# A four-layer graph network: the second layer's boundary rows put at their nodes by one-hots on chip, and its last chunk worked off in parts

## The reference, cut to what matters

```python
xn = x * rsqrt(sum(x * x, -1) + eps)
att = beta[0] * sum(xn[row_index] * xn[col_index], -1)        # one number per edge
m = segment_max(att, row_index)
e = exp(att - m[row_index])
denom = segment_sum(e, row_index)
alpha = e / maximum(denom[row_index], 1e-16)
out = segment_sum(alpha[:, None] * x[col_index], row_index)   # [6250, 64]
x = layernorm(x + out)
```

## Time and profile before

| what | value |
|---|---|
| runs | 4829.73, 4836.84, 4835.64 us; median 4835.64 us |
| the profiled execution | 4837.0 us, its span 4835.0 us |
| busy share of the span | POOL 73%, DVE 58%, PE 30%, ACT 23% |
| second layer, edge stage | 1201 to 2258 us |
| second layer, mend and node stage | 2258 to 2399 us |
| third layer, edge stage | 2399 to 3560 us |
| fourth layer, edge stage | 3706 to 4758 us |

### The profile page before, as it was taken

One profiled execution on the slowest core, in us unless ns is written; L12 is line 12 of the kernel. 1 busy time (PEld: TensorE's weight loads), 2 busy tenths in 40 slices (PEclk: granted clock), 3 DMA queues, 4 the chain that ended last, 5 costly groups with the idle time before them and its releaser, 6 DMA issues.

```text
span 4835.0 us, 31278 instructions
## 1 busy us (share of the span) xinstructions
PE 1465.4 (30%) x6525; PEld 744.2 (15%) x6525; DVE 2821.7 (58%) x7339; ACT 1123.2 (23%) x3417; POOL 3549.3 (73%) x3637
## 2 busy tenths in 40 slices
PE   7722100000000000000588888888834010000003
PEld 3611100000000000000233333333324010000002
DVE  4688632224555555555368888888866444444445
ACT  2200000000000000000278888888844000000000
POOL 6777777777777777776777777777734777777776
PEclk9855555555555555555799999999966555555555
DMA  7222222221222222222135555555532222222222
GB/s 279 72 95 96 86 78 79 79 73 50 69 80 80 80 80 80 80 80 60 59 124 213 196 199 213 191 203 213 199 137 61 78 78 78 78 78 78 79 78 75
DMA packets 185543, 529.64 MB, mean 110 GB/s; under 512 B 70422, under 2 KB 74634, under 8 KB 169080
## 3 DMA queue, kind: packets, MB, share of 16 engines
q1 hardware_dynamic: 65384, 395.51, 21.7%
q0 software_dynamic: 117728, 129.84, 11.7%
q10 hardware_dynamic: 2224, 2.13, 0.1%
HBM read 185.57 MB, written 341.47 MB: 109 GB/s over the span
## 4 chain that ended last, share of the span: by engine, by line
POOL 54%; issue 19%; DVE 9%; PE 7%; DMA 6%; ACT 4%; POOLq 0%; SPq 0%; DVEq 0%; ACTq 0%
POOL AR L190 52%; DMA AR<-xt,Si 4%; DVE AR L514 3%; POOL xd L194 2%; PE ps L680 2%; ACT AR L1306 2%; DMA AR<-y,R 1%; ACT AR L1168 1%; PE ps L1161 1%; PE ps L587 1%; PE ps L1177 1%; DVE AR L1290 1%; DVE AR L364 1%; DVE AR L366 1%; PE ps L372 0%
## 5 line engine op out<-in xcount | busy, mean ns | idle before, releaser
L190 POOL DMA_INDIRECT AR<-xt,Si x2496 | 2429.0, 973 | 809.6 <-issue 747.0
L190 POOL DMA_INDIRECT AR<-y,R x752 | 722.1, 960 | 237.4 <-issue 217.9
L1161 PE MATMUL ps<-AR,WLR 128*128 128x512 f32 x1248 | 626.8, 627 | 18.3 <-ACT AR L1168 18.3
L1320 DVE SCALAR_TENSOR_TENSOR AR<-AR,gf 128x390 f32<-128x390 f32 x780 | 484.6, 621 | 148.5 <-ACT AR L1306 132.7
L1306 ACT ACTIVATE AR<-AR 128x64 f32<-128x64 f32 x1664 | 498.5, 349 | 0.0
L514 DVE SCALAR_TENSOR_TENSOR AR<-AR,gf 128x64 f32<-128x64 f32 x831 | 237.4, 286 | 365.5 <-DMA AR<-y,R 337.6
L1595 DVE TENSOR_TENSOR AR<-AR,ps 128x2048 f32<-128x2048 f32 (+1 forms) x53 | 119.1, 2247 | 541.4 <-DMA AR<-xt,Si 541.4
L1168 ACT ACTIVATE AR<-ps 128x512 f32<-128x512 f32 x624 | 370.9, 595 | 80.5 <-PE ps L1161 78.4
L958 PE MATMUL ps<-AR,ones 128*128 128x384 f32 (+1 forms) x6 | 3.7, 759 | 1201.1 <-DVE AR L910 1201.1
L797 DVE TENSOR_TENSOR AR<-AR,ps 128x512 f32<-128x512 f32 x104 | 66.9, 684 | 443.9 <-DMA AR<-xt,Si 443.9
L1605 DVE SCALAR_TENSOR_TENSOR AR<-AR,gf 128x128 f32<-128x128 f32 x831 | 294.0, 354 | 29.5
(11 more groups left out here) (308 smaller groups left out, 2895.1 us busy)
## 6 DMA issues: line engine op xcount, KB each, us to landing
s<-AR SPq DMA_DIRECT2D x51, 3168.0 KB, 10.7
AR<-xd SPq DMA_DIRECT2D x104, 512.0 KB
s<-AR SPq DMA_DIRECT2D x51, 1024.0 KB, 4.0
AR<-xt,Si POOLq DMA_INDIRECT x2496, 2.5
s<-AR SPq DMA_DIRECT2D x52, 528.0 KB, 3.1
s<-AR SPq DMA_DIRECT2D x53, 512.0 KB, 2.7
xd<-AR SPq DMA_DIRECT2D x52, 512.0 KB
y<-AR SPq DMA_DIRECT2D x24, 1024.0 KB, 4.1
```

What stands on the lines that cost most here:

```text
L190: g.indirect_dma_start(out=o, out_offset=None, in_=table, in_offset=bass.IndirectOffsetOnAxis(ap=idx, axis=0)).then_inc(S[sem], 16)
L1161: t.matmul(PS[2 + k % 3][:], WLR[:, ch * P:(ch + 1) * P], XT2[:, u % 6, :], start=True, stop=True).then_inc(S["pm"], 1)
L1320: m = v.scalar_tensor_tensor(out=Sv[:, j, 0:HW], in0=Sv[:, j - 1, 0:HW], scalar=gf[:, c * CH + j:c * CH + j + 1], in1=Sv[:, j, 0:HW], op0= ...
```

## The change

`mend_soft_g` is split. The second layer keeps only the row gather, and its node gathers follow it in POOL's queue. The node rows of partition-crossing nodes are replaced on chip: `ends_v` makes, in the edge stage at chunk 20, one-hots of the partition's first node (`KE`, `LOE`) and the mask `has1` of the node slots that have a mended row; `ended_v` spreads the mended row over the slots, `ended_t` moves it with `KE` to the partition that owns the node, `ended_a` copies it from PSUM, and `nodes1_v` puts it over the gathered row with a predicated copy. In the last chunk the second half of the gathers has its own semaphore, the steps of the chunk before it run ahead of its `soft1` work, and it is stored in four parts of 4 columns. The third layer keeps its scatter. Counts of semaphores are adapted.

```diff
--- before.py
+++ after.py
@@ -61,13 +61,13 @@
 
 
 
-    late = 16 * CH // 2 if L and b == (NCH - 1) % N0 else 0
+    late = 16 * CH // 2 * min(L, 2) if b == (NCH - 1) % N0 else 0
     return sum(16 * CH // h * len(range(b // h, NCH, n)) for n, h in ((N0, 1), (4, 1), (NX, 2), (4, 1))[0:L] if b // h < n) - late
 
 
 def stored_before(L, b):
 
-    late = (16 if L and b == (NCH - 1) % N0 else 0) + (48 if L > 2 and b == (NCH - 1) % 2 else 0)
+    late = sum(m for l, (m, n) in enumerate(((16, N0), (48, 3), (48, 2))[0:L]) if b == (NCH - 1) % n)
     return sum(16 * len(range(b, NCH, n)) for n in (N0, 3, 2, 3)[0:L] if b < n) + late
 
 
@@ -111,7 +111,7 @@
                  "zrow"]
         names += [f"f{k}{n}" for k in range(2) for n in ("v", "io", "cn", "pe", "pos", "sc", "ld", "zt", "xs")]
         names += [f"{n}{k}" for k in range(2) for n in ("hoh", "hpe", "cnt", "rv", "rp")]
-        names += ["tl", "late", "lin0", "lin3", "rz", "rt", "ra", "ry", "rb", "rc"]
+        names += ["el", "ep", "ec", "tl", "late", "lin0", "lin3", "rz", "rt", "ra", "ry", "rb", "rc"]
         names += [f"g_{i}" for i in range(2 * NX)] + [f"s_{i}" for i in range(N0)] + [f"x_{i}" for i in range(3)]
         names += [f"ys{i}" for i in range(4)] + [f"nod_{i}" for i in range(2)]
         S = {n: ctx.enter_context(nc.semaphore("k_" + n)) for n in names}
@@ -612,7 +612,7 @@
                     v.copy_predicated(o, m_, y).then_inc(S["rc"], 1)
 
         def stored_all(e, L, n):
-            more = (16, 0, 48, 16)[L]
+            more = (16, 48, 48, 16)[L]
             for b in range(n):
                 e.wait_ge(S[f"s_{b}"], stored_before(L, b) + 16 * len(range(b, NCH, n)) + (more if b == (NCH - 1) % n else 0))
 
@@ -755,7 +755,8 @@
             if c >= 4:
                 e.wait_ge(S["p1"], 2 * (c - 3))
             for j in range(CH):
-                gather(G1[:, c % 4, j * 65:(j + 1) * 65], xt1, Si[:, c * CH + j:c * CH + j + 1], f"g_{c % 4}")
+                gather(G1[:, c % 4, j * 65:(j + 1) * 65], xt1, Si[:, c * CH + j:c * CH + j + 1],
+                       "late" if c == NCH - 1 and j >= CH // 2 else f"g_{c % 4}")
 
         def x1_chunk(e, c):
             if c >= 3:
@@ -792,7 +793,9 @@
                 e.wait_ge(S["q1"], n)
             if i == 0:
                 e.wait_ge(S["f1"], 16 * (c + 1))
-                e.wait_ge(S[f"g_{c % 4}"], gathered_before(1, c % 4) + 16 * CH * (c // 4 + 1))
+                e.wait_ge(S[f"g_{c % 4}"], gathered_before(1, c % 4) + 16 * CH * (c // 4 + 1) - (16 * CH // 2 if c == NCH - 1 else 0))
+            if i == 1 and c == NCH - 1:
+                e.wait_ge(S["late"], 16 * CH)
             if i <= 1:
                 m = v.tensor_tensor(TM1[:, 8 * i:8 * i + 8, :], Gv[:, 8 * i:8 * i + 8, 0:D],
                                     PS[2 * (c % 2) + i][:].rearrange("p (j d) -> p j d", j=8), ALU.mult)
@@ -848,6 +851,54 @@
                                    scalar=gf[:, c * CH + j:c * CH + j + 1] if j else pf1[:, c % 2, CH:CH + 1],
                                    in1=Sv[:, j, 0:65], op0=ALU.mult, op1=ALU.add).then_inc(S["t1"], 1)
 
+
+
+
+        KE = arena(15400, P)
+        LOE = arena(15600, NL)
+        has1 = arena(15700, NL).bitcast(I32)
+        TL1 = arena(16000, NG, GN * 65)
+        CP1 = arena(20000, NG, GN * 65)
+        ramp1 = arena(15000, P)
+        upto1 = arena(15200, P)
+        ke, keq, kel = sm[:, 17:18], sm[:, 18:19], sm[:, 19:20]
+
+        def ends_v(e, c):
+            c.hold()
+            v.tensor_scalar(ramp1, ident[:], pf, None, op0=ALU.mult).then_inc(S["el"], 1)
+            c.then(lambda: v.tensor_tensor(ke, df_, inv, ALU.subtract))
+            e.wait_ge(S["ep"], 1)
+            c.then(lambda: v.tensor_scalar(upto1, PS[5][:, 0:P], float(NL), ke, op0=ALU.mult, op1=ALU.is_le))
+            c.then(lambda: v.reduce_sum(keq, upto1, AX))
+            c.then(lambda: v.tensor_scalar(keq, keq, -1.0, None, op0=ALU.add))
+            c.then(lambda: v.tensor_scalar(KE, PS[5][:, 0:P], keq, None, op0=ALU.is_equal))
+            c.then(lambda: v.tensor_scalar(kel, keq, -float(NL), ke, op0=ALU.mult, op1=ALU.add))
+            c.hold()
+            v.tensor_scalar(LOE, lo64[:, 0:NL], kel, None, op0=ALU.is_equal).then_inc(S["el"], 1)
+            e.wait_ge(S["ep"], 2)
+            c.then(lambda: v.tensor_scalar(has1, PS[5][:, P:P + NL], 0.5, None, op0=ALU.is_gt))
+
+        def ends_t(e):
+            e.wait_ge(S["el"], 1)
+            t.matmul(PS[5][:, 0:P], ones[:], ramp1, start=True, stop=True).then_inc(S["ep"], 1)
+            e.wait_ge(S["el"], 2)
+            t.matmul(PS[5][:, P:P + NL], KE, LOE, start=True, stop=True).then_inc(S["ep"], 1)
+
+        def ended_v(e, q):
+
+            fr = mend_tiles(1, 14000)[0]
+            v.tensor_tensor(TL1[:, q, :].rearrange("p (l d) -> p l d", l=GN),
+                            bc(LOE[:, q * GN:(q + 1) * GN].unsqueeze(2), [P, GN, 65]),
+                            bc(fr[:, 0:65].unsqueeze(1), [P, GN, 65]), ALU.mult).then_inc(S["el"], 1)
+
+        def ended_t(e, q):
+            e.wait_ge(S["el"], 3 + q)
+            t.matmul(PS[q][:, 0:GN * 65], KE, TL1[:, q, :], start=True, stop=True).then_inc(S["ep"], 1)
+
+        def ended_a(e, q):
+            e.wait_ge(S["ep"], 3 + q)
+            s.copy(CP1[:, q, :], PS[q][:, 0:GN * 65]).then_inc(S["ec"], 1)
+
         def layer1_v(e):
             for j in range(CH):
                 fill1(e, 0, j)
@@ -861,6 +912,10 @@
                 at = 0
                 for j in range(CH):
                     step1(e, c, j)
+                    if c == 20 and j == 0:
+                        ends_v(e, vc)
+                    if c == NCH - 2 and j < CH - 1:
+                        continue
                     while at * CH < (j + 1) * beside:
                         if at < 9:
                             soft1(e, c + 1, at)
@@ -882,9 +937,11 @@
             for c in range(NCH):
                 if c + 3 < NCH:
                     x1_chunk(e, c + 3)
-                e.wait_ge(S["t1"], 16 * c + 15)
                 e.wait_ge(S["q1"], q1_at(c + 1))
-                load(e, chunk_view(s1, c), S1[:, c % 3, :], f"s_{c % 3}")
+                n = CH // 4 if c == NCH - 1 else CH
+                for j in range(0, CH, n):
+                    e.wait_ge(S["t1"], 16 * c + j + n - 1)
+                    load(e, columns_view(s1, c * CH + j, n), S1[:, c % 3, j * 66:(j + n) * 66], f"s_{c % 3}")
 
 
 
@@ -947,7 +1004,8 @@
                                  bc(w2.unsqueeze(2), [P, heads, 65]), ALU.mult))
             c.then(lambda: v.tensor_tensor(frv, frv, tv, ALU.add))
             c.hold()
-            v.tensor_copy(mr, Mx).then_inc(S["fr"], 1)
+            if L == 2:
+                v.tensor_copy(mr, Mx).then_inc(S["fr"], 1)
 
         def mend_soft_t(e, L, heads, base):
             aw = heads * 65
@@ -969,12 +1027,9 @@
             s.activation(w1, w1, ACT.Exp).then_inc(S["ma"], 1)
             s.activation(w2, w2, ACT.Exp).then_inc(S["ma"], 1)
 
-        def mend_soft_g(e, L, st, heads, base, nbuf):
-            fr = mend_tiles(heads, base)[0]
+        def mend_row_g(e, L, st, heads, base, nbuf):
             stored_all(e, L, nbuf)
-            gather(fr, st[:], fixg[:], "rowg")
-            e.wait_ge(S["fr"], L)
-            scatter(st[:], fr, fixs[:], "rows")
+            gather(mend_tiles(heads, base)[0], st[:], fixg[:], "rowg")
 
 
 
@@ -985,7 +1040,7 @@
         eto = arena(28600, 2, 512)
         WP = arena(30000, 2, 3 * P)
         VP = arena(30800, 2, 32)
-        K1 = 12
+        K1 = 13
         T1 = S1[:, (NCH - 1) % 3, :].rearrange("p (j d) -> p j d", j=CH)[:, CH - 1, :]
 
         def nodes1_v(e, q):
@@ -993,6 +1048,9 @@
             sl = slice(q * GN, (q + 1) * GN)
             c = n1c
             e.wait_ge(S[f"nod_{q % 2}"], 1 * 16 * GN * len(range(q % 2, NG, 2)) + 16 * GN * (q // 2 + 1))
+            e.wait_ge(S["ec"], q + 1)
+            c.then(lambda: v.copy_predicated(nb[:, :, 0:65], bc(has1[:, sl].unsqueeze(2), [P, GN, 65]),
+                                             CP1[:, q, :].rearrange("p (l d) -> p l d", l=GN)))
             c.then(lambda: v.tensor_scalar(den, nb[:, :, D], 1e-16, None, op0=ALU.max))
             c.then(lambda: v.reciprocal(den, den))
             c.then(lambda: v.tensor_tensor(nb[:, :, 0:D], nb[:, :, 0:D], bc(den.unsqueeze(2), [P, GN, D]), ALU.mult))
@@ -1591,7 +1649,7 @@
                 e.wait_ge(S[f"s_{c % 3}"], stored_before(3, c % 3) + 16 * (c // 3))
             for k in range(0, CH, n):
                 if k:
-                    e.wait_ge(S["late"], 16 * CH)
+                    e.wait_ge(S["late"], 16 * CH + 16 * CH // 2)
                 m3c.then(lambda: v.tensor_tensor(cur[:, k:k + n, :].rearrange("p j (b d) -> p j b d", b=NBS),
                                                  bc(buf[:, k:k + n, :].unsqueeze(2), [P, n, NBS, D]),
                                                  bc(CW3[:, :, k:k + n].rearrange("p b j -> p j b").unsqueeze(3), [P, n, NBS, D]),
```

(21 more changed lines are left out.)

## The result

The changed kernel takes 4813.6 us (median of five, 4806.8 to 4817.5) against 4835.6: ratio 0.9956, interval 0.9945 to 0.9968. Its profiled execution took 4814.8 us, its span 4812.9. That is 22 us faster, where 12.0 were forecast and the range ended at 4818. This kernel and its variants take 4755 to 4846 us in some executions and 6059 to 6257 in others, and a time is only set against times of its own kind.

What follows compares the result with a forecast made beforehand. POOL's queue of gathers was taken as the bound, so the first node gather's time decides. Gains 3.37 + 0.83 + 7.84 = 12.04 us, from the median 4835.6, gave 4823.6 us (0.25% faster), range 4818 to 4832.

Steps and rivals of the forecast that it cites:

- Part A: End of second layer's edge stage: last chunk in parts, chunk 50's steps first; last step ends 3.4 us earlier.
- the store: Last chunk's running sums stored in four parts: the last lands in 1.85 us, 0.83 us gained, bounds 0 and 0.9.
- Part B: Second layer, row gather to node gathers: mended rows stay on chip, 1.25 us instead of 9.09, 7.84 us gained.
- the cover: Second layer's first node group: done 1.7 us before POOL needs it, so the added on-chip work costs nothing.
- POOL slowed in the node stage: Second layer's node stage: fourteen more DVE passes could lose 1.0 us; taken as 0, 1.0 kept for the range.
- the sign that was named as wrong: Node stage: POOL issues of 1.2 us and more beside the predicated copies would show the forecast wrong.
- The exception for tensor_tensor: Node stage: tensor_tensor is excepted from DVE's lock on GpSimd descriptor writing; rows were said to agree for the spreads.
- POOL is shut out while DVE works: Rival, node stage: 14 added passes (0.62 us) each stop POOL's issuing; 8.7 us given back, 4832.3 us; chance 0.06.
- nothing in it depends on when it starts: Third layer: the argument against a loss of 3 to 6 us there from a different phase.
- The third layer gives part of it back: Rival, third layer: a different phase of its chunks or launch costs 3 to 6 us, 4827 to 4830; chance 0.14.
- a ring of PE, ACT, DVE and POOL: Third layer: chunks paced by gathers and engines together; POOL, PE and DVE each 73 to 84% busy.
- The rival on the clock: Third layer: PE's granted clock drops from 0.95 to about 0.93, 21 us more busy time, 4845 us; chance 0.04.

Runs made afterwards that it cites:

- warm_b3: The kernel before plus two 256-wide products, results thrown away, ahead of the third layer's gather wait: 4842.3 us, 1.0004 of before.
- warm_a3: The changed kernel plus two 256-wide products, results thrown away, ahead of the third layer's gather wait: 4814.0 us, 0.9948 of before.
- warm_b: The kernel before plus two thrown-away 256-wide products ahead of the third layer's gather wait, in the slow kind of execution: 6131.9 us.
- order: The changed kernel with chunk 50's steps spread over chunk 51's softmax work as before the change, slow kind of execution: 0.9980 of before.

## Why the prediction was right and wrong

- **Part A and the store.** Forecast 3.37 + 0.83. Measured 18.77 - 14.45 = 4.32 us together, of which the store is 0.93 (it lands 1.75 us after its last step, near the 1.85 taken), and the steps 3.39. Right. The Trainium skill's 2.0 us of fixed cost (page DMA: Bandwidth & Descriptors, section Anatomy of one DMA) would have put the store at 0.68; the trace, 1.75 us, lies below it.
- **Part B.** Forecast 7.84, measured 9.09 - 1.25 = 7.84. Right, and the cover held: products 7.08 us against 6.98, the last copy done 12.2 us behind the row gather's issue (forecast 12.0), and the group in time by 1.1 us (forecast 1.7).
- **POOL slowed in the node stage.** I took 0 from the earlier trace rows and kept 1.0; the stage is 0.5 us longer. The reading was at fault: the spreads in the earlier trace rows read `LOH,ps`, one input in PSUM, the added ones (L890) read SBUF twice, and beside the predicated copies POOL's issues take up to 1.43 us, the sign that was named as wrong. The exception for tensor_tensor that the prediction cites from the Trainium skill (page SBUF — State Buffer) does not hold here: two gathers beside L890 take 1.39 and 1.32 us. The rival "POOL is shut out while DVE works" had this mechanism, but priced it for the 14 added passes alone. Its price, 0.62 us each time, was too high (0.45 is the most seen beside such a pass), and its place was wrong: the wide SBUF passes beside POOL stand in the third layer, 780 of them.
- **The third layer, the step that failed.** The sum let it stand at its old length, because "nothing in it depends on when it starts", and the rival "The third layer gives part of it back" knew one sign only. Its edge gathers took 13.1 us less, all of it in the duration of the issues. I had called the layer paced by a ring of PE, ACT, DVE and POOL from the busy shares in the earlier trace rows; the group of its gathers, with idle that is all issue, would have said POOL, and a mean of 1022 ns against 940 in quiet stretches would have said that 67 us of collisions are in play. A swing of a fifth of that, either way, belonged into the range. That the time came out on the fast side of it was luck: nothing in the forecast spoke for fewer collisions.
- **The rival on the clock** looked at a quantity that moved (0.95 to 0.96) and that costs nothing here. It was wrong in its price, busy time over clock: that holds only where PE sets the pace.

What is shown: collisions of gather issues with L1320 are the third layer's whole difference (taken away in both kernels, it goes). What is only argued: why the changed kernel has fewer. A gather issued before the pass begins is free, one 0.1 us behind it costs 0.4 us, and one in 16 of the gathers (206 of 3328) lies within 0.05 us of a pass's start, so hundredths of a microsecond decide; the pattern then repeats from chunk to chunk (in the changed kernel runs of chunks of 20.7 us, before many of 21.2 to 21.3). That the difference belongs to the program and not to one launch is shown by the medians: 22 us apart in one comparison, 28 in another (warm_b3, warm_a3), with ten and four runs that don't overlap; the third layer's share of it, 13.1 and 12.1 us, is read from one trace of each kernel. Not tried: a kernel that holds the pass and the gathers apart on purpose.

## What to carry to other kernels

Ask of each long stage which engine's idle is all "issue", and multiply its instruction's excess over its quiet duration by the count, before calling the stage rigid: here 832 x 0.08 us hid 67 us in plain sight. Where POOL's indirect gathers set the pace, DVE passes of 0.6 us with two SBUF inputs beside them cost up to 0.45 us per collision, those of 0.3 us up to 0.06, those with an input in PSUM nothing; keep them short, or let them read PSUM (the second was not tried here). And a difference in a clock that is of the right size is no cause until taking it away moves the time.

## What was not expected of the hardware

- A gather issued during a DVE pass with both inputs in SBUF ends 0.82 us after the pass, 1.39 us long at most beside L1320; issued less than 0.05 us after the pass's start it takes its 0.94 in 60 of 62 cases.
- PE fell to 1.2 GHz after idles of 1.3 to 2.9 us in the third layer, and after none of 222 idles of 1.4 us between blocks of back-to-back products.
- Where the kernel before takes 6093 to 6229 us instead of 4835 to 4845, engines stand still between instructions: ACT idles 482.6 us before the 48 copies of L1188 in warm_b, 41.1 before 50 of the same copies in the kernel before (L1185). The second layer's edge stage grows by a sixth (1042 to 1224 us in order), the third layer's by half. Two chips gave both kinds, at different times; the cause is not known.
